# Where the square roots of the second feed-forward are taken: ScalarE or GpSimd

## The chip, the cores and the metric

One core of a Trainium2 chip runs the whole program. The metric is the device time of one launch in microseconds (us). TensorE (PE), VectorE (DVE), ScalarE (ACT) and GpSimd (POOL) each work through an instruction list of their own; SyncE (SP) issues most of the DMAs. They meet at semaphores.

## The reference

Two transformer layers on x of shape 4 x 1024 x 128, 16 heads of width 8. Layer 0 has attention by distances and a routed feed-forward. Layer 1, which the change touches, is:

```python
xn = _layernorm(x)
x = x + _L1_attn_ref(xn, ...) + _L1_ffn_ref(xn, ...)

# _L1_attn_ref: softmax(q k / sqrt(8)) over l, einsum 'blmh,blhd->blhd', out projection
# _L1_ffn_ref:
real = jnp.einsum('bti,io->bto', x, jnp.cos(theta + theta_noise))
imag = jnp.einsum('bti,io->bto', x, jnp.sin(phi + phi_noise))
return jnp.sqrt(real * real + imag * imag)
```

In the attention of layer 1 each query's value is multiplied by its own sum of weights, so only the row sums of the exponentials are wanted.

## The kernel before

The program has a long first part, 16 rounds of four heads of layer 0 (to about 975 us of the span), and then the attention of layer 1, which is one long loop: 4 batches b of 128 tiles s (16 heads x 8 blocks of 128 queries), 512 tiles in all. For each tile

- PE makes 128 x 1024 scores in one of three PSUM ring tiles (L1327),
- ACT takes the exponential into one of eight places `EX[k // 2][:, k % 2]` in SBUF (L1352, or L1348, which also makes the sum itself: every fifth tile, s = 16, 21, 26 and so on, outside the last batch),
- DVE folds the 1024 columns to a sum (L1360, `dve_fold`, "fold" below): both halves of the place are its inputs, so it reads two operands from SBUF. Tiles whose sum ACT makes have no fold.

`act_exp1` waits, at even s, until the folds of all tiles up to s - 7 are done: a place of EX is used again only then. PE can be three tiles ahead of ACT.

Beside this loop batch b + 1 is prepared while batch b runs, each step fixed to a tile number s by hand (`ATURN_AT`, `ADD_AT` and so on): DVE copies and adds at s = 20 and 30, adds the feed-forward of layer 0 at s = 31 to 46 (L1190 and L1199, one short instruction a tile, two operands from SBUF plus a scalar), measures and normalises, keeps q, k, v, and copies real and imaginary parts to `ri` at s = 114 and 126 (`dve_square_mix`). POOL gathers rows by indirect DMA (`pool_gather`), takes the deviation, splits q into parts (`pool_split_q1`) and squares and adds `ri` into `mag[b]` (`pool_powers`, twice a batch, L1302 and L1304). Batch 0 is prepared in the last round of layer 0. At the end of a batch the output projection of the attention is added: PE begins it at s = 36 of the next batch (`FWO_AT`), in the one PSUM tile `aux`, which DVE's step at s = 30 (`dve_add_att`, L1183) has to have emptied, and its first instructions are two matmuls for the bias (L1163). DVE adds the result at s = 40.

The roots are taken by `act_magnitudes`: at s = 16 of the last batch (`MAG_HEAD` = 2 heads of 8 tiles) ACT turns from exponentials to roots, takes four roots of 128 x 1024, and turns back. `pool_add_magnitudes` adds `mag[b]` to `X[b]` for each batch. Those of batches 0 and 1 follow at once, those of 2 and 3 after the projection of batch 2 (s = 40). SP stores the results of batches 0 to 2 from s = 55 on; DVE needs the last sum at s = 122.

In layer 0 POOL already takes some of the square roots by nine fp32 operations (`pool_roots`, L771 to L786): an integer seed, one multiplication, and a cubic, in place. Its DVE partner there reads PSUM.

Which of the two branches runs (`by_guard`) is decided by the data; the trace shows the fast one.

Of the kernel before, what the change touches and what calls it, by code (L numbers as in the profile page):

```python
# [19 lines left out]
I32 = mybir.dt.int32  # L20
# [5 lines left out]
P = 128  # L26
# [209 lines left out]
def build(nc, d):  # L236
    with ExitStack() as ctx, ExitStack() as scores_ctx, ExitStack() as room:
# [43 lines left out]
        with ExitStack() as own:  # L281
            late_room = lambda n, s, t=F32: own.enter_context(nc.sbuf_tensor(n, s, t))
            EX = [late_room(f"exp{i}", [P, 2, N]) for i in range(NT // 2)]
            X = [None] + [late_room(f"X{b}", [P, NT, D]) for b in range(1, B)]
            V1 = [None] + [late_room(f"V{b}", [P, NT, D]) for b in range(1, B)]
            mag = [None] + [late_room(f"mag{b}", [P, NT, D]) for b in range(1, B)]
            fatt = late_room("fatt", [P, N])

# [239 lines left out]
        def pool_deviation(pool, n, ready, done):  # L530
            pool.wait_ge(ready, n + 1)
            nc.gpsimd.tensor_tensor(rstd[:], mv[:, :, 1], power.to_broadcast([P, NT]), ALU.pow).then_inc(done, 1)  # L532
# [929 lines left out]
        def act_magnitudes(act):  # L1462
            for b in range(B):
                act.wait_ge(mag_half, 2 * (b + 1))
                nc.scalar.activation(mag[b][:, :, :], mag[b][:, :, :], ACT.Sqrt).then_inc(mag_root, 1)

        def pool_add_magnitudes(pool, o, b, after_end):
            pool.wait_ge(mag_root, b + 1)
            if after_end:
                o.emptied(pool, ("fwo", b))  # L1470
            else:
                pool.wait_ge(xn1_ready, NT * (b + 1))
            nc.gpsimd.tensor_tensor(X[b][:, :, :], X[b][:, :, :], mag[b][:, :, :], ALU.add).then_inc(mag_added, 1)
# [119 lines left out]
        FTURN_AT, ATURN_AT, AWO_AT, FWO_AT = 10, 18, 26, 36  # L1593
        ADD_AT, STATS1_AT, NORMAL_AT, TURN1_AT = 31, 47, 57, 68
        Q1_AT, K1_AT, SPLIT1_AT, V1_AT, MIX_AT = 79, 88, (92, 94, 96, 98), 97, (108, 120)
        MAG_HEAD, STORE1_HEAD, STORE_RESULT_HEAD = 2, 12, 6

        WEIGH_LAST_AT = [LAST_GROUP + GROUP * hi for _, hi in LAST_PARTS[:-1]]
        TURN_LAST_AT, KEEP_LAST_AT = [WEIGH_LAST_AT[0] + 4, H * NT - 2], [WEIGH_LAST_AT[0] + 5, H * NT - 4]
# [384 lines left out]
        @block.scalar  # L1984
        def _(act):
            act.dma_start(early["full"][:], d["early_full"]).then_inc(early_in, 16)
            act.dma_start(limit["full"][:], d["limit_full"]).then_inc(limit_in, 16)
            for i, (a, b) in enumerate((("theta", "theta_noise"), ("phi", "phi_noise"))):
                act.dma_start(ang[:, i, :], d[a]).then_inc(angles_in, 16)
                act.dma_start(noise[:, i, :], d[b]).then_inc(angles_in, 16)  # L1990
            act_first(act, first_order)

            def sines(act):
                act.wait_ge(reduced, 1)
                nc.scalar.activation(cs0[:].rearrange("p (a c) -> p a c", a=2), ang[:, :, :], ACT.Sin
                                     ).then_inc(trig_done, 1)

            def general(act):
                sines(act)
                general0(act, "act")  # L2000
                act_odds(act)
                for v in range(FIRST_JOBS, LAST_JOBS + 1):
                    act_tanh(act, general_order, v)
                act_magnitudes(act)
                for u in range(GROUPS):
                    general1(act, "act", u)

            def fast(act):
                o = fast_order
                sines(act)  # L2010
                for r in range(GROUPS):
                    if r:
                        for place in range(GROUP):
                            act_root_halves(act, o, r, place) if (r, place) == (1, GROUP - 1) else act_root(act, o, r, place)
                    else:
                        act_first_roots(act, o)
                    for place in range(GROUP):
                        if place == 2:
                            if r == FIRST_JOBS - 1:
                                act_odds(act)  # L2020
                            if FIRST_JOBS <= r <= LAST_JOBS:
                                act_tanh(act, o, r)
                        act_exp0(act, r, place) if r or place else act_first_exp(act)
                for b in range(B):
                    for s in range(H * NT):
                        if b == B - 1 and s == MAG_HEAD * NT:
                            act_magnitudes(act)
                        act_exp1(act, o, b, s)

            by_guard(act, general, fast)  # L2030

        @block.gpsimd
        def _(pool):
# [49 lines left out]
            def fast(pool):  # L2083
                o, chain, roots = fast_order, Chain(pool, pool_steps, 1), Chain(pool, newton_steps)
                store_sines(pool)
                pool_deviation(pool, 1, var_ready, std_ready)
                normalise0(pool, nc.gpsimd, 1)
                for r in range(GROUPS):
                    if 1 <= r < B:
                        pool_qk0(pool, o, chain, r)  # L2090
                        if r + 1 < B:
                            pool_deviation(pool, r + 1, var_ready, std_ready)
                            normalise0(pool, nc.gpsimd, r + 1)
                        if r == 1:
                            pool_roots(pool, o, roots, r, 1)
                        pool_sums0(pool, o, chain, r)
                    if FIRST_JOBS < r <= LAST_JOBS + 1:
                        pool_hidden(pool, r - 1)
                    if r == PLACE_ROUND:
                        pool_place(pool, o, chain)  # L2100
                    if r == ADD1_ROUND:
                        pool.wait_ge(y_stored, Y_ALL)
                        pool_gather(pool, 0)
                    if r == PLACE_ROUND + 1:
                        pool_scatter(pool, 2)
                        for place in range(1, GROUP - 1):
                            pool_roots(pool, o, roots, r, 1, place - 1, place)
                            pool.wait_ge(att_ready, GROUP * (r - 1) + place + 1)
                            pool_scatter(pool, 2 + place)
                    elif r == PLACE_ROUND + 2:  # L2110
                        pool_scatter(pool, 7)
                    if r > 1 and r != PLACE_ROUND + 1:
                        pool_roots(pool, o, roots, r, 1)
                    if r == FIRST_JOBS or r > PLACE_ROUND + 1:
                        pool_roots(pool, o, roots, r, 2, 0, 1)
                    if r:
                        pool_store_out(pool, r - 1)
                    if r == PLACE_ROUND:
                        pool_scatter(pool, 0)
                    if r == PLACE_ROUND + 1:  # L2120
                        pool_scatter(pool, 5)
                    if r == ADD1_ROUND:
                        pool_deviation(pool, 0, var1, std1)
                    if r == 2:
                        pool_roots(pool, o, roots, r, 2)
                    elif r > PLACE_ROUND + 1 or r == FIRST_JOBS:
                        pool_roots(pool, o, roots, r, 2, 1)
                    if FIRST_JOBS < r <= LAST_JOBS + 1:
                        pool_store_jobs(pool, o, r - 1)
                    if r == PLACE_ROUND:  # L2130
                        pool_scatter(pool, 1)
                    if r == PLACE_ROUND + 1:
                        pool_scatter(pool, 6)
                    pool_roots(pool, o, roots, r, 3)
                    if r == TURN1_ROUND:
                        roots.wait()
                        clear_stacks1(pool)
                pool_split_q1(pool, o, chain, 0)
                for i in range(2):
                    pool_powers(pool, o, chain, 0, i)  # L2140
                pool_store_out(pool, GROUPS - 1)
                pool.wait_ge(att_out, 32 * GROUPS)
                for b in range(1, B):
                    pool_gather(pool, b)
                    pool_deviation(pool, b, var1, std1)
                    pool_split_q1(pool, o, chain, b)
                    for i in range(2):
                        pool_powers(pool, o, chain, b, i)
                for b in range(B):
                    pool_add_magnitudes(pool, o, b, b < B - 1)  # L2150

# [299 lines left out]
```

## Time and profile before

| | us |
|---|---|
| median of 3 runs | 1465.37 (1465.34 to 1466.09) |
| profiled execution, its time | 1468.72 |
| profiled execution, its span | 1467.0 |
| ACT busy | 1428.0 (97%) |
| DVE busy | 1220.8 (83%) |
| PE busy | 1110.7 (76%) |
| POOL busy | 884.5 (60%) |

Times in the rows are counted from the start of the span. Durations overlap a little where an engine has one instruction in flight behind the other, so the distance between two starts says more than the durations. A timeline row of several instructions has its total and their number. In the layer 1 loop POOL is mostly idle and ACT is hardly ever.

### The profile page before, as it was taken

The page shows a single profiled execution, that of the slowest core. Times are in us where ns is not written, and L with a number is a line of the kernel's source. Part 1 is how long each engine was busy: PE and PEld are TensorE (multiplying, and loading weights), DVE is VectorE, ACT ScalarE, POOL GpSimd, SP SyncE. Part 2 cuts the span into 40 slices and gives each one's busy share as a digit, 9 for nine tenths or more (in the row PEclk, how much of TensorE's full clock was granted, in tenths as well). Part 3 has the DMA queues.
Part 4 walks back from the last instruction along what each step waited for, and adds up shares of the span by engine and source line. Part 5 has one row for each costly group of instructions (what it writes and reads, how often), then busy time and mean ns, then how long its engine had stood idle before and what let it go on. Part 6 is the DMA issues. An engine that isn't in the chain of part 4 may idle for free.

```text
span 1467.0 us, 22437 instructions
## 1 busy us (share of the span) xinstructions
PE 1110.7 (76%) x8231; PEld 445.9 (30%) x8260; DVE 1220.8 (83%) x2196; ACT 1428.0 (97%) x796; POOL 884.5 (60%) x656
## 2 busy tenths in 40 slices
PE   5587787888788888888887675777777677776766
PEld 2133224245143352452542311322223122221212
DVE  6998889978879879789788588838898898998886
ACT  3999999999999999999999999989999999999998
POOL 5188998878789898898898985933213023022100
PEclk8599988999999999899999897889999999999999
DMA  4942544222322235254353231034033033021020
GB/s 121 253 141 65 167 129 125 60 61 73 82 82 62 64 102 155 80 144 131 83 155 96 69 75 31 13 120 81 27 128 71 27 113 81 27 106 33 23 70 20
DMA packets 113185, 130.04 MB, mean 89 GB/s; under 512 B 42906, under 2 KB 81178, under 8 KB 113066
## 3 DMA queue, kind: packets, MB, share of 16 engines
q1 hardware_dynamic: 107738, 116.74, 29.5%
q0 software_dynamic: 4464, 11.09, 2.8%
q8 instruction: 67, 1.10, 0.3%
q10 hardware_dynamic: 864, 0.69, 0.2%
q14 instruction: 52, 0.43, 0.1%
HBM read 83.79 MB, written 44.70 MB: 88 GB/s over the span
## 4 chain that ended last, share of the span: by engine, by line
ACT 38%; POOL 27%; DVE 15%; issue 12%; PE 6%; DMA 2%; SPq 1%; ACTq 0%; DVEq 0%; POOLq 0%
ACT exp L1352 13%; ACT scores L830 11%; ACT scores L791 6%; DVE exp L1360 6%; DVE scores L737 6%; POOL scratch L775 3%; POOL scores L773 3%; ACT exp L1348 3%; PE pvb L718 3%; POOL gate L1098 3%; POOL scratch L784 3%; POOL scores L786 3%; POOL scratch L780 3%; ACT h L1091 2%; POOL scratch L777 1%
## 5 line engine op out<-in xcount | busy, mean ns | idle before, releaser
L737 DVE TENSOR_SCALAR scores<-ring 128x1024 f32<-128x1024 f32 x512 | 591.8, 1216 | 62.2 <-PE ring L703 58.9
L830 ACT ACTIVATE scores<-scores 128x8192 f32<-128x8192 f32 x63 | 438.9, 7020 | 0.2
L1352 ACT ACTIVATE exp<-ring 128x1024 f32<-128x1024 f32 x438 | 431.4, 1388 | 4.4 <-PE ring L1327 3.9
L718 PE MATMUL pvb<-scores,val 128*9 128x256 f32 x4096 | 338.3, 406 | 97.8 <-ACT scores L830 63.7
L1327 PE MATMUL ring<-stk 128*128 128x512 bf16 x995 | 300.9, 386 | 131.2 <-ACT exp L1352 103.4
L791 ACT ACTIVATE scores<-scores 128x7296 f32<-128x7296 f32 (+2 forms) x59 | 384.1, 6574 | 4.9 <-DVE scores L737 4.8
L1360 DVE SCALAR_TENSOR_TENSOR exp<-exp 128x512 f32<-128x512 f32 x438 | 322.3, 758 | 62.6 <-ACT exp L1352 55.6
L703 PE MATMUL ring<-stk 64*128 64x512 bf16 x1024 | 216.1, 419 | 59.2 <-DVE scores L737 45.4
L1327 PEld LDWEIGHTS ring<-stk 128*128 128x128 bf16 x1024 | 66.1, 97 | 341.7 <-ACT exp L1352 232.5
L703 PEld LDWEIGHTS ring<-stk 64*128 64x128 bf16 x1024 | 50.0, 94 | 303.4 <-DVE scores L737 182.3
L718 PEld LDWEIGHTS pvb<-scores,val 128*9 128x9 f32 x4096 | 65.8, 89 | 226.9 <-issue 223.5
L1059 PE MATMUL ring<-xjt,w 128*128 128x128 f32 x840 | 101.3, 285 | 10.9 <-issue 9.7
L1059 PEld LDWEIGHTS ring<-xjt,w 128*128 128x128 f32 x840 | 100.0, 201 | 12.3 <-issue 10.8
L1348 ACT ACTIVATE exp<-ring 128x1024 f32<-128x1024 f32 x74 | 100.0, 1354 | 0.2 <-PE ring L1327 0.2
L773 POOL TENSOR_TENSOR scores<-scores,scratch 128x896 f32<-128x896 f32 (+1 forms) x39 | 75.2, 1928 | 3.3
L784 POOL TENSOR_TENSOR scratch<-scratch 128x896 f32<-128x896 f32 (+1 forms) x39 | 75.2, 1927 | 3.3
L775 POOL TENSOR_TENSOR scratch<-scores,scratch 128x896 f32<-128x896 f32 (+1 forms) x39 | 75.2, 1929 | 3.1
L786 POOL TENSOR_TENSOR scores<-scores,scratch 128x896 f32<-128x896 f32 (+1 forms) x39 | 75.1, 1925 | 3.1
L1302 POOL TENSOR_TENSOR at<-at 128x1024 f32<-128x1024 f32 x8 | 17.4, 2176 | 93.2 <-DVE at L1298 93.2
L532 POOL TENSOR_TENSOR rstd<-mv,columns 128x8 f32<-128x8 f32 x7 | 11.7, 1674 | 100.7 <-DVE mv L528 100.7
L1084 DVE COPY h<-ring 128x384 f32<-128x384 f32 x70 | 39.0, 557 | 26.7 <-PE ring L1059 25.9
L780 POOL TENSOR_TENSOR scratch<-scratch 128x896 f32<-128x896 f32 (+1 forms) x39 | 60.3, 1546 | 0.0
(263 smaller groups left out, 1434.9 us busy)
## 6 DMA issues: line engine op xcount, KB each, us to landing
stk<-stack SPq DMA_DIRECT2D x192, 192.0 KB, 2.8
w<-in_w SPq DMA_DIRECT2D x39, 352.0 KB, 3.6
w<-in_w SPq DMA_DIRECT2D x39, 192.0 KB, 2.7
stack<-qp SPq DMA_DIRECT2D x7, 768.0 KB, 4.4
stack<-kp SPq DMA_DIRECT2D x7, 768.0 KB, 5.4
xj<-xg SPq DMA_DIRECT2D x10, 448.0 KB
yg<-xj POOLq DMA_DIRECT2D x10, 448.0 KB, 3.6
stack<-qp SPq DMA_DIRECT2D x7, 512.0 KB, 5.1
```

What stands on the lines that cost most here:

```text
L703: mm = nc.tensor.matmul(tile[:, cols], stk0[slot][side, K, j * P:(j + 1) * P], stk0[slot][side, Q, cols], start=True, stop=True)
L718: mm = nc.tensor.matmul(pvb[place % 2][32 * c:32 * c + VW, 0:256], val[place][:, j, :], S[place][:, j * N + c * 256:j * N + (c + 1) * 256] ...
L737: nc.vector.tensor_scalar(S[place][:, j * N:(j + 1) * N], tile, 1e-12, None, ALU.max).then_inc(o.release(("qk", group, place, j)), 1)
L773: chain.step(nc.gpsimd.tensor_tensor(x, x, y, ALU.mult))
L775: chain.step(nc.gpsimd.tensor_tensor(y, x, y, ALU.mult))
L791: nc.scalar.activation(part, part, ACT.Sqrt).then_inc(root_done, 1)
L830: nc.scalar.activation(S[place][:], S[place][:], ACT.Exp, scale=-1.0).then_inc(exp_done, 1)
L1059: mm = nc.tensor.matmul(tile[:, at_col:at_col + P], w13[:, slot_of(v, j), side, first:first + P], xjt[:, j * P:(j + 1) * P], start=True, s ...
L1327: mm = nc.tensor.matmul(out[:, cols], stk1[place][:, Q, i * P:(i + 1) * P], stk1[place][:, K, cols], start=True, stop=True)
L1348: nc.scalar.activation(EX[k // 2][:, k % 2, :], tile, ACT.Exp, scale=SCALE1, accum_out=den[n // GROUP % 2][:, n % GROUP, i:i + 1]).then_in ...
L1352: nc.scalar.activation(EX[k // 2][:, k % 2, :], tile, ACT.Exp, scale=SCALE1).then_inc(o.release(("qk1", n, i)), 1)
L1360: nc.vector.scalar_tensor_tensor(out=tile[:, k % 2, 0:N // 2], in0=tile[:, k % 2, 0:N // 2], scalar=1.0, in1=tile[:, k % 2, N // 2:N], op0 ...
```

## The change

ACT no longer takes the roots in the fast branch. POOL takes them by the nine operations of layer 0, now on whole tiles of 128 x 1024 with two scratch tiles of their own (8 KB a partition), each operation but one waiting for the one before. The roots of batch b - 1 stand between the gather and the deviation of batch b, those of the last batch after its powers and ahead of the four additions. POOL also waits there once for the last weighing matmuls of layer 0, whose SBUF space the scratch tiles share.

```diff
+            mag_y, mag_h = late_room("mag_y", [P, N]), late_room("mag_h", [P, N])
...
+        def pool_magnitudes(pool, chain, b):
+            pool.wait_ge(mag_half, 2 * (b + 1))
+            y, h, x = mag_y[:], mag_h[:], flat(mag[b])
+            chain.step(nc.gpsimd.tensor_scalar(y.bitcast(I32), x.bitcast(I32), -0.5, SEED_BITS, ALU.mult, ALU.add))
+            chain.wait()
+            chain.step(nc.gpsimd.tensor_tensor(x, x, y, ALU.mult))
+            chain.wait()
+            chain.step(nc.gpsimd.tensor_tensor(y, x, y, ALU.mult))
+            chain.wait()
+            chain.step(nc.gpsimd.tensor_scalar(h, y, CUBIC[0], 1.0, ALU.add, ALU.mult))
+            chain.wait()
+            chain.step(nc.gpsimd.tensor_scalar(y, y, CUBIC[2], CUBIC[3], ALU.add, ALU.mult))
+            chain.step(nc.gpsimd.tensor_tensor(h, h, h, ALU.mult))
+            chain.wait()
+            chain.step(nc.gpsimd.tensor_scalar(h, h, CUBIC[1], 1.0, ALU.add, ALU.mult))
+            chain.wait()
+            chain.step(nc.gpsimd.tensor_tensor(h, h, y, ALU.mult))
+            chain.wait()
+            nc.gpsimd.tensor_tensor(x, x, h, ALU.mult).then_inc(mag_root, 1)
...
-        MAG_HEAD, STORE1_HEAD, STORE_RESULT_HEAD = 2, 12, 6
+        STORE1_HEAD, STORE_RESULT_HEAD = 12, 6
...
-                        if b == B - 1 and s == MAG_HEAD * NT:
-                            act_magnitudes(act)
                         act_exp1(act, o, b, s)
...
                 pool.wait_ge(att_out, 32 * GROUPS)
+                pool.wait_ge(pv_done, CHG * GROUPS)
                 for b in range(1, B):
                     pool_gather(pool, b)
+                    pool_magnitudes(pool, roots, b - 1)
                     pool_deviation(pool, b, var1, std1)
                     pool_split_q1(pool, o, chain, b)
                     for i in range(2):
                         pool_powers(pool, o, chain, b, i)
+                pool_magnitudes(pool, roots, B - 1)
                 for b in range(B):
                     pool_add_magnitudes(pool, o, b, b < B - 1)
```

## Rows read from the trace of the kernel before

**Rows 1.** Busy time by engine in two stretches: window and length, engines, PEclk, DMA, GB/s
```profile
core 0: us, PE busy (x) PEld busy (x) DVE busy (x) ACT busy (x) POOL busy (x), PEclk, DMA share, GB/s
1095.00:1215.00 120.00, 89.83 (x357) 31.95 (x362) 106.49 (x280) 119.97 (x153) 25.93 (x17) 1.00 0.26 71
1351.00:1358.00 7.00, 0.65 (x3) 0.11 (x2) 1.45 (x6) 6.94 (x8) 4.25 (x2) 0.86 0.00 0
```

**Rows 2.** Timeline of ACT in the last batch: start, us, engine, line, operation
```profile
1338.72 12.57 ACT L1352 ACTIVATE exp<-ring 128x1024 f32<-128x1024 f32 x13
1351.32 1.28 ACT L1465 ACT_TABLE_LOAD   x1
1352.61 3.90 ACT L1465 ACTIVATE mag<-mag 128x1024 f32<-128x1024 f32 x4
...
1357.82 43.39 ACT L1352 ACTIVATE exp<-ring 128x1024 f32<-128x1024 f32 x47
```

**Rows 3.** Timeline of POOL, first two of the four splits of q, batch 1
```profile
1056.49 1.43 POOL L574 CAST qp<-ysh 128x1024 bf16<-128x1024 f32 x1 [22.44 <-DVE ysh L1244]
1058.01 2.45 POOL L576 TENSOR_TENSOR ysh<-ysh,qp 128x1024 f32<-128x1024 f32 x1
```

**Rows 4.** Timeline of DVE, the folds beside those splits and two after
```profile
1056.97 1.49 DVE L1360 SCALAR_TENSOR_TENSOR exp<-exp 128x512 f32<-128x512 f32 x1
...
1058.40 2.60 DVE L1360 SCALAR_TENSOR_TENSOR exp<-exp 128x512 f32<-128x512 f32 x1
...
1060.93 1.51 DVE L1360 SCALAR_TENSOR_TENSOR exp<-exp 128x512 f32<-128x512 f32 x1
...
1062.38 2.60 DVE L1360 SCALAR_TENSOR_TENSOR exp<-exp 128x512 f32<-128x512 f32 x1
...
1064.91 0.68 DVE L1360 SCALAR_TENSOR_TENSOR exp<-exp 128x512 f32<-128x512 f32 x1
...
1065.52 0.68 DVE L1360 SCALAR_TENSOR_TENSOR exp<-exp 128x512 f32<-128x512 f32 x1
```

**Rows 5.** Timeline of POOL, the additions of batches 2 and 3
```profile
1383.05 5.42 POOL L1473 TENSOR_TENSOR X<-X,mag 128x1024 f32<-128x1024 f32 x2 [24.66 <-DVE X L1414]
```

**Rows 6.** Timeline of DVE, the first fold beside those additions
```profile
1383.44 2.83 DVE L1360 SCALAR_TENSOR_TENSOR exp<-exp 128x512 f32<-128x512 f32 x1
```

**Rows 7.** Timeline of POOL where DVE has no fold to make
```profile
953.90 1.03 POOL L574 CAST qp<-ysh 128x1024 bf16<-128x1024 f32 x1
...
960.44 1.89 POOL L1302 TENSOR_TENSOR at<-at 128x1024 f32<-128x1024 f32 x1
...
1353.74 4.64 POOL L1473 TENSOR_TENSOR X<-X,mag 128x1024 f32<-128x1024 f32 x2 [12.17 <-ACT mag L1465]
```

**Rows 8.** Groups by form, POOL, a scalar step of the nine in layer 0
```profile
L771 POOL TENSOR_SCALAR scratch<-scores 128x896 int32<-128x896 int32 x32 | 30.0, 937 | 13.6 <-DVE scores L737 9.6 <-issue 1.6
```

**Rows 9.** Timeline of POOL, the instructions that the nine follow (batches 0, 1, 3)
```profile
1010.95 1.25 POOL L1139 DMA_INDIRECT yro<-yg,pos  x1 [0.30 <-issue]
...
1112.62 1.40 POOL L1139 DMA_INDIRECT yro<-yg,pos  x1 [0.30 <-issue]
...
1340.02 1.56 POOL L1304 TENSOR_TENSOR mag<-at 128x512 f32<-128x512 f32 x1
```

**Rows 10.** Timeline of DVE where the nine come to lie in batches 0 and 1
```profile
1012.18 0.35 DVE L1190 SCALAR_TENSOR_TENSOR X<-ysh,WT,X 128x128 f32<-128x128 f32 x1
1012.45 0.69 DVE L1360 SCALAR_TENSOR_TENSOR exp<-exp 128x512 f32<-128x512 f32 x1
...
1114.61 0.69 DVE L1360 SCALAR_TENSOR_TENSOR exp<-exp 128x512 f32<-128x512 f32 x1 [0.79 <-issue]
...
1127.35 1.22 DVE L1183 TENSOR_TENSOR X<-X,aux 128x1024 f32<-128x1024 f32 x1
```

**Rows 11.** Timeline of ACT: tile 46 of batch 0, tiles 37 to 40 of batch 1
```profile
1021.17 1.21 ACT L1348 ACTIVATE exp<-ring 128x1024 f32<-128x1024 f32 x1
...
1132.38 3.77 ACT L1352 ACTIVATE exp<-ring 128x1024 f32<-128x1024 f32 x4
```

**Rows 12.** Groups by form, PE, the bias matmuls in `aux`
```profile
L1163 PE MATMUL aux<-late_rows,fixed_full 128*128 128x512 f32 x26 | 12.4, 596 | 0.7 <-DVE fatt L1433 0.7
```

## The prediction

> **What bounds the kernel now.** I read the busy times by stretch first. From 1095 to 1215 us, one batch of the layer 1 loop, ACT is busy 119.97 of 120 us [rows 1]: the loop ends when ACT has made its 512 exponentials, so a microsecond taken from ACT is won, and one in which it waits is lost for good. DVE is busy 106.49 of the same 120 us and POOL 25.93: POOL has room by its own time, DVE has little. Then the timeline of ACT in the last batch shows the detour that the change removes [rows 2]. Last I read POOL and DVE side by side wherever POOL is busy in this loop [rows 3 to 6], because the nine operations must run there.
>
> **What is removed.** Tiles 3 to 15 of the last batch are the 13 exponentials from 1338.72 us. The 47 after the detour take 43.39 us, that is 0.92 us a tile. Tile 16 would start at 1338.72 + 13 x 0.917 = 1350.6 us and starts at 1357.82 [rows 2]. The detour costs 7.2 us: two table loads of 1.3 us, four roots in 3.90 us, and 0.7 us for the pipe. PE has nothing to do meanwhile and its granted clock falls (mean 0.86 in that window, so for part of it at 1.2 and not at 2.4 GHz, [rows 1]), but the 47 exponentials keep their pace, so the clock adds nothing. Sum so far: -7.2 us.
>
> The Trainium skill (ScalarE: Activation LUTs, What ACT_TABLE_LOAD costs) gives 2.66 us for each change of table, 1.28 of it the load and the rest a drain. By it the detour would be 2 x 2.66 + 3.90 = 9.2 us and the gain 2 us more. The trace agrees on the load, but shows 7.2 us in all; I go by the trace.
>
> **What is added: POOL's time.** Alone, an fp32 sum of two tiles takes 4.64 / 2 = 2.32 us, a square 1.89, a one-operand CAST 1.03 [rows 7]; the scalar steps of the nine take 0.937 at 896 columns [rows 8], so about 1.05 at 1024, next to the cast. Nine operations are four scalar steps, one square and four two-operand ones: 4.2 + 1.9 + 4 x 2.32 = 15.4 us a batch, without gaps. POOL has that time: in batch 0 from 1012.3 us on, in batches 1 and 2 from 1114.2 us and one batch later, in batch 3 from 1341.7 [rows 9]. The gathers stand ahead of the nine, so no DMA is later, and the wait for layer 0's matmuls adds nothing behind the wait for their stored result. Were that all, the change would win 7.2 us.
>
> **What is added: DVE's folds wait.** It isn't all. Beside a cast of POOL a fold takes 1.49 us and beside a two-operand step 2.60, against a start-to-start distance of 0.61 in folds that have POOL to themselves [rows 3, 4]. POOL's operation grows too: cast 1.03 to 1.43, pair of sums 4.64 to 5.42 [rows 3, 5, 7], where the fold takes 2.83 [rows 6]. So they take turns: each POOL operation runs whole, one fold gets in behind it, then the next operation. In the 7.9 us of the four splits DVE makes four folds [rows 4], where ACT needs about seven in that time. Turns hold for any DVE instruction with two SBUF operands, I take it: the short L1190 too.
>
> The Trainium skill (SBUF — State Buffer, Who interferes with whom) states the rule that speaks against this change: a VectorE instruction with two SBUF inputs and a GpSimd one that reads SBUF exclude each other for their whole length. It says that issue order decides, not that they alternate; were VectorE to win several turns in a row, the loss below would shrink towards the second rival.
>
> With turns, a fold lengthens the period by 0.4 to 0.45 us, a short L1190 by about 0.2. The chain of nine takes 15.4 + 9 x 0.43 = 19.3 us beside folds and lets through nine or ten DVE instructions. ACT makes 21 tiles in that time and can run ahead of the folds by 6 or 7. The four splits stayed within this slack; nine don't.
>
> *Batch 0.* The chain starts at 1012.4 us; DVE is at the fold of tile 34 [rows 9, 10]. It lies among the short additions, one a tile, so it gets through 34, add, 35, add, add (36 has no fold), 37, add, 38, add: nine turns. Half of them lengthen the period by 0.2 only, so the chain ends at 1012.4 + 15.4 + 4 x 0.45 + 5 x 0.2 = 1030.6, and fold 39, for which tile 46 waits, is done near 1031.4. Tile 46 starts at 1021.17 now [rows 11]: +10.2 us.
>
> *Batches 1 and 2.* The chain starts at 1114.2 us, fold 17 waits for it [rows 9, 10]. Turns: 17, 18, 19, 20, 22, 23, 24, 25; one turn is lost to the PSUM copy at tile 20, which needs none. The chain ends near 1132.8, folds 25, 27 to 30 are done at 1135.9, and only then comes L1183 (tile 30), which now starts at 1127.35 [rows 10]. It ends at 1137.1. PE stands at tile 36 until it has, then makes two bias matmuls of 0.6 us [rows 12] and the scores of tile 37, 0.6 us. Tile 37 starts near 1139 instead of 1132.38 [rows 11]: +6.6, and PE, now without lead, has the projection's matmuls among the next four tiles: I take +7 in each batch, +14 in both.
>
> *Batch 3.* The last L1304 ends at 1341.6 us [rows 9], the chain runs from 1342.0 to 1361.2 beside folds 1 to 9, and the additions of batches 0 and 1 follow, which lie in ACT's detour now [rows 7]: two more turns of 2.8 us, folds 10 and 11, done near 1367.3. Tile 18 waits for fold 11. Without the detour it would start at 1350.6 + 1.8 = 1352.5: +14.8, and the copy at tile 12 adds 0.6: +15.4.
>
> *Sum:* -7.2 + 10.2 + 14 + 15.4 = +32.4 us. The profiled span would be 1467.0 + 32.4 = 1499.4. The profiled execution's 1468.72 lies 3.35 above the median; the loss being the same on both, I predict 1465.37 + 32.4 = 1497.8 us. What is late next is DVE, with a backlog of six tiles after each chain; it clears it at 0.61 us a fold against 0.92 (more slowly beside the additions), before the steps at tile 57 and later, where PE needs its results. The deviation, behind the nine in POOL's list, now comes at tile 55, when the chain is over.
>
> **Bounds.** From below, the trace doesn't show whether a scalar step that is no cast shares turns with the fold. Nearest above is the cast, which does; I take that. If it doesn't, see the second rival. From above, each stall may be a tile or two longer: one more turn is up to 2.8 us in any of four batches, and PE's clock falls in each (it did in 7 us, [rows 1]) while in batches 0 to 2 PE has projections to make. Two turns and 1.5 us of slow PE in three batches are +10: 1508.
>
> **Rivals.** (1) *Faster.* All turns fit in the slack of ACT: decided where a chain leaves at most about six tiles unfolded. The four splits do fit [rows 4]; the nine would have to last under 12 us, or fold and POOL overlap. Then only -7.2 remains: 1458.2 us. Against it stand rows 3 to 6.
> (2) *Smaller loss.* The four scalar steps let folds pass, or DVE gets two folds in per turn. In 4.2 us a chain DVE makes up to seven folds, not four; with shorter periods that is some 4.5 us less stall a chain, 18 us in four: 1479.8 us.
> (3) *Larger loss.* PE, idle in each stall and slow after it, holds ACT further, or the backlog reaches the next step's deadline (q, k at tile 79 on): another +10 to +20, about 1512 us.
> (4) *It doesn't show:* the roots on POOL cost just what they save. This needs a loss of 7 us in four chains, under 2 each; nothing in the rows gives it.
>
> **How the numbers follow.** Forecast 0.72, (2) 0.15, (3) 0.08, (1) 0.04, (4) 0.01. The range runs from 1478 (rival 2) to 1508 (upper bound) and leaves (3), (1) and (4) out. About 0.2% (2.9 us) is what a measurement of this kernel tells from no change. Faster 0.04, same 0.01, slower 0.95.
>
> **What the profile would show.** ACT: no table load near 1351 us, but gaps or stretched starts behind each chain, in order 10, 7, 7 and 15 us. DVE: folds of 2.8 us beside POOL's two-operand steps, about 1.5 beside scalar steps, nine turns a chain. POOL: chains of 18 to 20 us; the granted clock dips once a batch. Wrong would be: folds of 0.7 us beside scalar steps (rival 2), no gap of ACT at all (rival 1), gaps that don't follow the chains (rival 3).

## The result and the profile after

The changed kernel takes 1495.24 us (median of 4, 1493.47 to 1497.07) against 1465.47 (median of 4) in the same session: ratio 1.0205, 95% interval 1.0193 to 1.0217, so 29.8 us slower. Its profiled execution has 1493.47 us and a span of 1491.8, 24.8 above the span before. It happens to be the fastest of its four runs, while the profiled execution before (1468.72) lies above all of its timed ones, so the two spans understate the difference.

The page's busy times are the first hint. POOL worked 74 us more than before (884.5 then), DVE 49 us more (1220.8 then) with the same 2196 instructions, ACT 6 us less:

```profile
PE 1124.5 (75%) x8260; PEld 445.7 (30%) x8260; DVE 1269.4 (85%) x2196; ACT 1422.3 (95%) x790; POOL 958.8 (64%) x692
```

An engine that gets busier with the same work is being held inside its instructions, and that is DVE here. What ACT waited for from just ahead of the layer 1 loop to its end (engine and line, released by, us in total, times, longest), the changed kernel:

```profile
ACT exp L1353 <- DVE exp L1361: 18.4, 9, 3.6
ACT exp L1353 <- PE ring L1328: 14.4, 6, 5.6
ACT exp L1349 <- DVE exp L1361: 2.7, 1, 2.7
ACT exp L1349 <- PE ring L1328: 0.2, 1, 0.2
```

and the kernel before:

```profile
ACT exp L1352 <- PE ring L1327: 3.9, 2, 2.1
ACT exp L1348 <- PE ring L1327: 0.2, 1, 0.2
```

Waits on DVE's folds were not there at all; waits on PE were 4.1 us. To place them I measure the loop by ACT's own sums, of which each batch has its first at tile 16 and its last at tile 121. These are the readings of the accumulator in the timeline of the changed kernel, tiles 16 and 121 of batch 0, the same of batches 1 and 2, and the last sum of all (the line numbers are one higher than before):

```profile
989.13 0.26 ACT L1349 ACTIVATION_READ_ACCUMULATOR exp<-ring 128x1 f32 x1
1094.92 0.65 ACT L1349 ACTIVATION_READ_ACCUMULATOR exp<-ring 128x1 f32 x1
1115.81 0.92 ACT L1349 ACTIVATION_READ_ACCUMULATOR exp<-ring 128x1 f32 x1
1220.95 0.64 ACT L1349 ACTIVATION_READ_ACCUMULATOR exp<-ring 128x1 f32 x1
1241.84 0.92 ACT L1349 ACTIVATION_READ_ACCUMULATOR exp<-ring 128x1 f32 x1
1346.97 0.65 ACT L1349 ACTIVATION_READ_ACCUMULATOR exp<-ring 128x1 f32 x1
1485.66 0.24 ACT L1349 ACTIVATION_READ_ACCUMULATOR exp<-ring 128x1 f32 x1
```

and three of the kernel before, the first, tile 121 of batch 2 and the last:

```profile
993.93 0.26 ACT L1348 ACTIVATION_READ_ACCUMULATOR exp<-ring 128x1 f32 x1
1330.49 0.64 ACT L1348 ACTIVATION_READ_ACCUMULATOR exp<-ring 128x1 f32 x1
1461.51 0.24 ACT L1348 ACTIVATION_READ_ACCUMULATOR exp<-ring 128x1 f32 x1
```

From such rows, in us (batch 3 from tile 121 of batch 2 to the last sum; "between" the two stretches from tile 121 to the next tile 16):

| | batch 0 | batch 1 | batch 2 | batch 3 | between | loop |
|---|---|---|---|---|---|---|
| before | 97.85 | 98.47 | 98.47 | 131.02 | 41.77 | 467.58 |
| changed | 105.79 | 105.14 | 105.13 | 138.69 | 41.78 | 496.53 |
| difference | +7.9 | +6.7 | +6.7 | +7.7 | 0 | +28.95 |

The whole difference of the medians, 29.8 us, lies in this loop but for 0.8. What lies around the loop (median minus the loop of the profiled execution) is 997.9 and 998.7 us. From one profiled execution to another tile 16 of batch 0 comes at 989 to 995 us, which is why spans are a poor measure here and this table is a good one: where nothing disturbs them, batches 1 and 2 repeat to 0.1 us and batch 0 to 0.4.

Batch 1 shows what happens. The chain on POOL:

```profile
1117.27 1.05 POOL L1471 TENSOR_SCALAR mag_y<-mag 128x1024 int32<-128x1024 int32 x1
1118.40 2.67 POOL L1473 TENSOR_TENSOR mag<-mag,mag_y 128x1024 f32<-128x1024 f32 x1
1121.14 2.68 POOL L1475 TENSOR_TENSOR mag_y<-mag,mag_y 128x1024 f32<-128x1024 f32 x1
1123.91 1.37 POOL L1477 TENSOR_SCALAR mag_h<-mag_y 128x1024 f32<-128x1024 f32 x1
...
1132.86 2.68 POOL L1486 TENSOR_TENSOR mag<-mag,mag_h 128x1024 f32<-128x1024 f32 x1
```

and DVE beside it:

```profile
1117.75 1.10 DVE L1361 SCALAR_TENSOR_TENSOR exp<-exp 128x512 f32<-128x512 f32 x1 [0.75 <-ACT exp L1353]
...
1118.78 2.83 DVE L1361 SCALAR_TENSOR_TENSOR exp<-exp 128x512 f32<-128x512 f32 x1
...
1121.55 2.83 DVE L1361 SCALAR_TENSOR_TENSOR exp<-exp 128x512 f32<-128x512 f32 x1
...
1124.31 1.51 DVE L1361 SCALAR_TENSOR_TENSOR exp<-exp 128x512 f32<-128x512 f32 x1
...
1125.75 1.21 DVE L1158 COPY att_t<-aux 128x1024 f32<-128x1024 f32 x1
```

One DVE instruction gets in for each operation, here eight folds and one copy for the nine. A fold takes 0.68 us alone; beside an operation it is held until that operation is done: 2.83 us beside two operands, 1.51 beside a scalar step. These are the turns of [rows 3, 4] and [rows 6]. The last row is the surprise. PE needs this copy (tile 20) for the output projection of layer 0 at tile 26, and it starts 9.9 us after ACT's sum of tile 16 (1115.81), where it started 5.3 us after it before (1117.91 against 1112.66). PE and ACT, the same batch:

```profile
1127.02 3.78 PE L1164 MATMUL aux<-late_rows,fixed_full 128*128 128x512 f32 x4 [3.13 <-DVE att_t L1158]
```

```profile
1131.69 3.92 ACT L1353 ACTIVATE exp<-ring 128x1024 f32<-128x1024 f32 x4 [5.62 <-PE ring L1328]
...
1142.19 3.77 ACT L1353 ACTIVATE exp<-ring 128x1024 f32<-128x1024 f32 x4 [0.92 <-PE ring L1328]
```

ACT stops at tile 27, not at tile 34 or 37, with nothing wrong in the folds it waits for. The bias matmuls (two in the program, four rows in the profile) took 3.78 us. The same four of the kernel before, with the clock at full speed:

```profile
1120.58 1.88 PE L1163 MATMUL aux<-late_rows,fixed_full 128*128 128x512 f32 x4
```

PE had idled for 3.1 us, and from 1127 to 1131 us its granted clock was 0.50, the level of 1.2 GHz:

```profile
1127.00:1131.00 4.00, 3.98 (x5) 1.47 (x6) 4.00 (x5) 0.00 (x0) 3.83 (x3) 0.50 0.02 4
```

(columns as in [rows 1]). From the first bias matmul to ACT's tile 27 it is 4.67 us here and was 2.35 before (1120.58 to 1122.93): the clock lengthens this stall by 2.3 us.

Batch 3, the additions included, is the plain case of folds. ACT:

```profile
1347.06 15.22 ACT L1353 ACTIVATE exp<-ring 128x1024 f32<-128x1024 f32 x16
1365.66 1.94 ACT L1353 ACTIVATE exp<-ring 128x1024 f32<-128x1024 f32 x2 [3.38 <-DVE exp L1361]
1368.54 1.94 ACT L1353 ACTIVATE exp<-ring 128x1024 f32<-128x1024 f32 x2 [0.95 <-DVE exp L1361]
1372.28 1.94 ACT L1353 ACTIVATE exp<-ring 128x1024 f32<-128x1024 f32 x2 [1.80 <-DVE exp L1361]
1377.78 1.94 ACT L1353 ACTIVATE exp<-ring 128x1024 f32<-128x1024 f32 x2 [3.56 <-DVE exp L1361]
1383.28 1.94 ACT L1353 ACTIVATE exp<-ring 128x1024 f32<-128x1024 f32 x2 [3.56 <-DVE exp L1361]
```

Two exponentials, then a wait of two turns, again and again: ACT runs at the pace of POOL.

### The profile page after: what moved, and what is told of

It is laid out like the page before. It is cut to its first block, busy times and chain, and to the rows that moved or that the text cites. A ratio compares the mean times of both kernels' runs of the same rounds, so it can differ in the third digit from the quotient of the medians.

```text
span 1491.8 us, 22496 instructions
## 1 busy us (share of the span) xinstructions
PE 1124.5 (75%) x8260; PEld 445.7 (30%) x8260; DVE 1269.4 (85%) x2196; ACT 1422.3 (95%) x790; POOL 958.8 (64%) x692
## 4 chain that ended last, share of the span: by engine, by line
ACT 52%; DVE 20%; issue 12%; PE 7%; POOL 6%; DMA 1%; SPq 0%; another core or an unknown queue 0%; ACTq 0%; DVEq 0%; POOLq 0%
ACT scores L831 18%; ACT scores L792 16%; ACT exp L1353 11%; DVE exp L1361 10%; DVE scores L738 6%; PE pvb L719 3%; ACT exp L1349 3%; PE ring L704 2%; ACT h L1092 2%; ACT L831 1%; ACT L792 1%; DVE X L1191 1%; POOL scores L774 1%; POOL scratch L776 1%; PE ring L1328 1%
## 5 line engine op out<-in xcount | busy, mean ns | idle before, releaser
L1328 PE MATMUL ring<-stk 128*128 128x512 bf16 x1024 | 313.3, 393 | 132.8 <-ACT exp L1353 107.1
L1361 DVE SCALAR_TENSOR_TENSOR exp<-exp 128x512 f32<-128x512 f32 x438 | 363.0, 857 | 39.7 <-ACT exp L1353 36.0
L1060 PE MATMUL ring<-xjt,w 128*128 128x128 f32 x840 | 98.2, 279 | 10.6 <-issue 9.5
L1060 PEld LDWEIGHTS ring<-xjt,w 128*128 128x128 f32 x840 | 96.8, 196 | 12.1 <-issue 10.5
L1099 POOL TENSOR_TENSOR gate<-gate,h 128x2688 f32<-128x2688 f32 x10 | 59.4, 5942 | 0.9
```

What stands on the lines that cost most here:

```text
L1060: mm = nc.tensor.matmul(tile[:, at_col:at_col + P], w13[:, slot_of(v, j), side, first:first + P], xjt[:, j * P:(j + 1) * P], start=True, s ...
L1328: mm = nc.tensor.matmul(out[:, cols], stk1[place][:, Q, i * P:(i + 1) * P], stk1[place][:, K, cols], start=True, stop=True)
L1361: nc.vector.scalar_tensor_tensor(out=tile[:, k % 2, 0:N // 2], in0=tile[:, k % 2, 0:N // 2], scalar=1.0, in1=tile[:, k % 2, N // 2:N], op0 ...
```

## The experiments

All times beside the kernel before on the same chip (its medians there 1465.1 to 1466.0 us). "Loop" is the last column of the table above, for each run's profile.

**Nothing in place of the roots.** The chains are left out.

```diff
                     pool_gather(pool, b)
-                    pool_magnitudes(pool, roots, b - 1)
...
-                pool_magnitudes(pool, roots, B - 1)
```

> The changed kernel with the nine operations left out: nobody takes the roots of the second feed-forward, and the four additions of POOL stay. It measures what taking the detour from ACT is worth when nothing comes in its place. Theory (turns between POOL's operations and DVE's folds make the loss): only the 7.2 us of the detour go, ratio to the kernel before 0.995, about 1458 us, and ACT shows no gap longer than before. Rival (the detour was not worth 7.2 us, or removing it already upsets the loop): 1465 us or more.

Measured: 1461.63 us, ratio 0.9978 (0.9968 to 0.9987), loop 463.48. Faster, but by 3.5 us in the medians and 4.1 in the loop, not by the 7.2 that the theory gave. Batches 0 to 2 are those of before to 0.15 us; batch 3 has 127.05. ACT, batch 3:

```profile
1343.87 1.94 ACT L1353 ACTIVATE exp<-ring 128x1024 f32<-128x1024 f32 x2 [1.01 <-DVE exp L1361]
1347.23 101.14 ACT L1353 ACTIVATE exp<-ring 128x1024 f32<-128x1024 f32 x110 [1.43 <-DVE exp L1361]
```

The additions of batches 0 and 1, which the detour used to cover, now come right behind the powers of batch 3, four reading operations in a row, and that already costs ACT 2.4 us. So a kernel without the detour comes near the 7.2 us only if the additions find another place.

**The same time on POOL, without reading.**

```diff
-            chain.step(nc.gpsimd.tensor_scalar(y.bitcast(I32), x.bitcast(I32), -0.5, SEED_BITS, ALU.mult, ALU.add))
...
-            nc.gpsimd.tensor_tensor(x, x, h, ALU.mult).then_inc(mag_root, 1)
+            for k in range(12):
+                chain.step(nc.gpsimd.memset(mag_y[:], 0.0))
+                chain.wait()
+            nc.gpsimd.memset(mag_h[:], 0.0).then_inc(mag_root, 1)
```

> The changed kernel with each chain of nine operations replaced by 13 memsets of 128 x 1024 (1.15 us each in this kernel's rows, so 15 to 16 us a chain, the time that the nine would need alone), in the same places with the same waits; the roots are not taken. POOL is busy and late by as much, but reads nothing from SBUF. Theory (what stops DVE is an operation of POOL that reads SBUF while the fold reads two operands): folds keep 0.68 us beside the memsets and the time is that without the nine, about 1458 us. Rival (POOL being busy, whatever it does, delays the loop, by its queue or by any access to SBUF): folds of 1.5 us beside the memsets; with 13 turns a chain the loss is at least that of the changed kernel, 1495 us or more.

Measured: 1458.48 us, ratio 0.9948 (0.9932 to 0.9965), loop 461.10, that is 6.5 us less than before. POOL and DVE in batch 1:

```profile
1111.43 12.08 POOL L1471 MEMSET mag_y<- 128x1024 f32 x12
```

```profile
1113.77 0.69 DVE L1361 SCALAR_TENSOR_TENSOR exp<-exp 128x512 f32<-128x512 f32 x1 [0.22 <-ACT exp L1353]
...
1114.68 0.69 DVE L1361 SCALAR_TENSOR_TENSOR exp<-exp 128x512 f32<-128x512 f32 x1 [0.21 <-ACT exp L1353]
...
1115.30 1.22 DVE L1158 COPY att_t<-aux 128x1024 f32<-128x1024 f32 x1
```

The memsets came out at 1.0 us each, so a chain is 13 us, and not the 15 to 16 that were expected (the nine take 18.3 in the changed kernel), but no fold beside them is longer than 0.69. POOL being busy for 13 us more in each batch cost nothing; reading does. This is the decisive run. The Trainium skill (SBUF — State Buffer, Who interferes with whom) says just this, that a GpSimd instruction which only writes doesn't meet a two-operand VectorE one. It also gives what the detour is worth by the end of batch 3: 124.41 us here, 6.6 less than before.

**Operation by operation, spread over the tiles.**

```diff
+        def pool_spread(pool, o, chain, steps, b, places):
+            for s in places:
+                o.emptied(pool, ("qk1", *tile_at(b, s)))
+                chain.wait()
+                chain.step(next(steps))
...
-                    pool_magnitudes(pool, roots, b - 1)
+                        pool_spread(pool, o, roots, steps[1], 1, (18, 25))
```

> All roots are taken on POOL by the same nine operations, but one at a time: those of batch 0 ahead of the loop (scratch in ysh and yro), the other 27 each behind a tile of the loop, six in batch 1, six in batch 2, fifteen in batch 3, with six to eight tiles or more between most of them, and the additions likewise. Theory (a POOL operation delays the folds by 1 to 2 us, and ACT loses only when the backlog passes about six tiles): folds of 1.5 to 2.8 us appear singly, no ACT gaps of several us, so the detour's 7.2 us are won: 1458 to 1461 us, ratio 0.995 to 0.997. Rival (each POOL operation costs ACT time wherever it stands, 29.6 + 7.2 = 37 us for 36 operations, about 1 us each): near 1490 us.

Measured: 1474.7 us, ratio 1.0062 (1.0045 to 1.0079), loop 473.29. Twenty microseconds of the loss are gone with the same 36 operations, so an operation has no fixed price. But neither is it free, and the forecast missed by 14 us: batches 1 and 2 have 102.68 and 103.36 us, with all of the excess at tiles 102 to 111, behind two operations (tiles 97 and 104) that met DVE's split of k; batch 3 has 127.84, 3.4 over the memset run; and what lies around the loop is 1001.4 us instead of 997.5 in that session (see below, e8_spread_more).

**The copy at tile 20 moved ahead of the chain.**

```diff
-                            if s == ATURN_AT:
+                            if s == ATURNS_AT[b]:
...
+        ATURNS_AT = [18, 13, 13]
```

> The changed kernel, with the transposition of the attention's output of layer 0 and its copy by DVE moved from tiles 18 and 20 to tiles 13 and 15 in batches 1 and 2, so that the copy is made before the chain of nine starts at about tile 16. It tells apart what ACT waits for in these two batches. Theory (several limits lie close together: the copy at tile 20, the folds seven tiles back, the emptying of aux at tile 30): the PE gap of 3.1 us before the bias matmuls at tile 26 goes, the loss moves to the next limit, tiles 34 to 37, and the sum stays within 1.5 us of the changed kernel a batch, 1492 to 1495 us. Rival (the copy at tile 20 alone makes the loss of 6.7 us a batch): about 13 us less, 1482 us.

Measured: 1496.99 us, ratio 1.0215 (1.0198 to 1.0232), loop 500.80. It lies 2 us above its forecast and far from the rival's 1482, but it doesn't answer cleanly. The transposition at tile 13 needs `aux` from DVE's step at tile 12, and DVE still has the backlog of the powers there:

```profile
1115.42 1.12 PE L1150 MATMUL aux<-fixed_full,at 128*128 128x128 f32 x4 [3.41 <-DVE fatt L1398]
```

That wait is new: 25.05 and 24.15 us between the batches instead of 20.89. Inside batches 1 and 2 the loss is 4.2 and 5.8 us instead of 6.7. ACT's long wait at tile 27 went, and waits of 0.7 to 1.5 us at tiles 26, 28, 30 and 37 came (in batch 2 three of 1.3 to 3.0 us).

**The chain moved behind the copy.**

```diff
                     pool_gather(pool, b)
+                    if b > 1:
+                        o.emptied(pool, ("aturn", b))
                     pool_magnitudes(pool, roots, b - 1)
```

> The changed kernel, but in batches 1 and 2 POOL waits with the nine until DVE has made its copy at tile 20 (the copy for which PE was seen to wait before the bias matmuls at tile 26). This tells apart again what the stall in these batches hangs on; the first try moved the copy and brought a wait of its own. Theory (the stall is the backlog of DVE, and whichever of its duties is due next shows it): the wait moves to the aux tile at tile 36 or to the folds, and a batch loses 5 to 9 us still, 1494 to 1500 us in all. Rival (the copy at tile 20 alone): the loss of 6.7 us a batch falls under 2, about 1485 us.

Measured: 1499.06 us, ratio 1.0231 (1.0214 to 1.0248), batches 1 and 2 at 108.30 and 106.94 us: 9.8 and 8.5 us lost instead of 6.7. This is the clean test of the same question. PE, batch 1:

```profile
1140.80 3.78 PE L1164 MATMUL aux<-late_rows,fixed_full 128*128 128x512 f32 x4 [6.42 <-DVE X L1184]
```

The wait sits at tile 36 for DVE's step at tile 30, the place that the prediction had named, and is longer; the bias matmuls behind it are again at half the pace. The copy at tile 20 isn't the cause, only the first duty that the backlog makes late.

**Twice as many instructions, half as long.**

```diff
+            cut = [slice(width * k, width * (k + 1)) for k in range(PIECES)]
+            ts, tt = nc.gpsimd.tensor_scalar, nc.gpsimd.tensor_tensor
-            chain.step(nc.gpsimd.tensor_tensor(x, x, y, ALU.mult))
+            chain.step(each(lambda c: tt(x[:, c], x[:, c], y[:, c], ALU.mult)))
```

> The changed kernel with each of the nine operations and each of the four additions cut into two of half the columns, in the same places. POOL moves the same bytes in twice the instructions and is busy longer. Theory (POOL and DVE take turns by instruction, one fold gets in after each): 18 folds a chain in some 23 to 25 us instead of nine or ten in 19, so in batches 1 and 2, where 20 folds are needed in that time, the stall all but goes; batch 3 keeps 1 to 4 us; about 1460 to 1468 us. Rival (the loss follows POOL's busy time or its bytes, not its instruction count): as the changed kernel or more, 1495 to 1502 us.

Measured with PIECES = 2: 1483.37 us, ratio 1.0122 (1.0105 to 1.0139), loop 485.12: 11.4 us of the loss gone, though POOL's chain in batch 1 grew from 18.3 to 23.1 us. The rival fell, but the forecast missed by 15 us too. Batches 1 and 2 lose 2.9 us each (6.7 with whole operations), batch 3 10.9 over the 124.41 of the memset run (14.3) where 1 to 4 were expected, and batch 0, with 7.5 (7.9), gained almost nothing; why it didn't is not shown.

**Four times as many.** The same with PIECES = 4.

> The same with four pieces for each operation and addition, 256 columns each: 36 instructions a chain. Theory of turns by instruction: a fold gets in about every 1.0 to 1.1 us, against a need of one in 1.15 us in batches 1 and 2 and one in 0.92 in batch 3; no ACT gap of over 1 us anywhere, so the detour's 7.2 us are won: 1457 to 1461 us, faster than the kernel before. Rival (busy time or bytes): 1500 us or more. A second rival: short instructions let DVE in but cost POOL so much at 0.1 us or more apiece that the chain reaches the next duties of POOL (deviation at tile 55): 1465 or more.

Measured: 1475.23 us, ratio 1.0064 (1.0048 to 1.0081), loop 476.59, chains of 29.6 us in batch 1. It is better again, and the chain is 11 us longer than in the changed kernel: the loss follows the number of turns that DVE gets in a given time, not POOL's time. But it missed its forecast by 14 us. POOL, batch 1, and three folds beside it:

```profile
1122.11 3.99 POOL L1486 TENSOR_TENSOR mag<-mag,mag_y 128x256 f32<-128x256 f32 x4
```

```profile
1126.58 1.21 DVE L1361 SCALAR_TENSOR_TENSOR exp<-exp 128x512 f32<-128x512 f32 x1
...
1127.71 1.20 DVE L1361 SCALAR_TENSOR_TENSOR exp<-exp 128x512 f32<-128x512 f32 x1
...
1130.67 0.87 DVE L1361 SCALAR_TENSOR_TENSOR exp<-exp 128x512 f32<-128x512 f32 x1
```

A fold of 1.2 us is still longer than ACT's tile of 0.92, so in batch 3, where every tile has one, 7.6 us stay. Batches 1 and 2 lose 1.6 us each. And in batch 0, which loses 4.7, the second rival happened, at one place: the chain ended at 1041.8 us, the deviation behind it was late, and ACT has a gap of 3.4 us there.

**The spread placement mended.** Five operations each in batches 1 and 2, and ACT takes sums in the last batch too.

```diff
-    return n < HEADS - H and 12 <= s < 124 and s % 5 == 1 or n >= HEADS - GROUP and ...
+    return n < HEADS - GROUP and 12 <= s < 124 and s % 5 == 1 or n >= HEADS - GROUP and ...
```

> The spread kernel with its misplaced operations moved. It had lost 4.2 and 4.9 us in batches 1 and 2 at tiles 97 to 110, where an operation met DVE's split of k and the copy of v, and 4.4 in batch 3. Now five operations in each of batches 1 and 2, none between tiles 73 and 106, 17 operations and the additions in batch 3 at every fourth or fifth tile from 12 on, and ACT makes every fifth sum in batch 3 too (tiles to 95), which takes 17 folds from DVE. Theory (loss only where DVE's backlog passes what the next duty allows): no gap in batches 1 and 2, at most 2 us in batch 3: 1458 to 1462 us. Rival (each operation costs ACT about 0.3 us wherever it stands, the 36 of the first try having cost some 13 us): 1470 to 1475 us.

Measured: 1464.02 us, ratio 0.9989 (0.9979 to 0.9998), loop 463.46. Batches 0 to 2 have 97.61, 98.49 and 98.50 us, with the ten operations in batches 1 and 2 costing nothing; batch 3 has 127.12, 2.7 over the memset run, of which some 1.4 are ACT's 16 additional sums (an estimate, by the price of a sum in the next runs). So the loop won 4.1 us with all roots taken. The median won only 1.9, short of its forecast of 1458 to 1462 us: what lies around the loop is 1000.6 us instead of 998.4 in that session. The nine operations of batch 0 stand there, ahead of the loop. That they are the cause fits e11_spread_best, which has none there, and ACT's gaps at tiles 10 to 15 of batch 0, where the kernel before has none:

```profile
986.20 4.69 ACT L1355 ACTIVATE exp<-ring 128x1024 f32<-128x1024 f32 x5 [0.50 <-DVE exp L1363]
992.37 1.02 ACT L1355 ACTIVATE exp<-ring 128x1024 f32<-128x1024 f32 x1 [1.48 <-PE ring L1330]
```

**More sums on ACT, and their price.** In both runs `s % 3 == 1` instead of `s % 5 == 1`, up to tile 95 of the last batch; in the first the 36 operations all behind tiles of the loop, in the second nothing else.

> All roots on POOL again, operation by operation behind tiles of the loop, but none ahead of it (the nine of batch 0 ahead of the loop had delayed DVE's copy for the last group of layer 0: 0.5 and 1.5 us of ACT gaps before tile 16). ACT makes every third sum instead of every fifth, in all four batches (tiles 12 to 123, in the last to 95), which takes some 15 folds a batch off DVE (27 in the last) at under 0.1 us of ACT each. Six operations a batch from tile 66 on and three in the next batch at tiles 16, 20, 24. Theory (a POOL operation costs ACT nothing while DVE's backlog stays small): the 6.6 us of the detour are won and 2 to 4 us given for the sums: in the loop 462 to 466 us against 467.6, in all 1460 to 1463 us, faster than the kernel before. Rival (POOL's reads cost DVE and through it ACT in any place): 1466 us or more.

> The kernel before with nothing changed but that ACT makes every third sum instead of every fifth, as in the run above; the roots stay on ACT. It gives the price of the sums alone. Theory: ACT bounds the loop, each sum costs it under 0.1 us and folds taken from DVE win nothing: 1467 to 1469 us. Rival (DVE's share is what holds the loop in batches 0 to 2, and relief there wins time): 1463 us or less, and then what the run above wins is not the roots'.

Measured: 1466.98 us, ratio 1.0010 (1.0001 to 1.0019), and 1472.61 us, ratio 1.0053 (1.0040 to 1.0066). Both lie above their forecasts. The 73 additional sums cost 6.6 us, 0.09 us each. The price of one was as expected; the totals in the two forecasts (2 to 4 us, 1 to 3 us) were summed too low. So the spread kernel isn't faster than before. Between these two kernels, though, only the place of the roots (and of the additions) differs, and POOL's wins 5.6 us.

**All in the loop, sums as before.**

> The last placement: all 36 operations on POOL one by one behind tiles of the loop, none ahead of it, none between tiles 75 and 106 of a batch, ACT's sums every fifth tile as in the kernel before and in the last batch up to tile 95 too. Batches 0, 1 and 2 take 4, 6 and 6 operations, the last takes 20 and the four additions, one about every fourth tile. Theory: the loop costs as little as in e8_spread_more or 1 to 2 us more (463.5 to 465.5 us from the first sum of ACT to the last, against 467.6), and what lies ahead of it is 2 to 3 us shorter than there: 1461 to 1464 us, ratio to the kernel before 0.996 to 0.999. Rival (24 actions in the last batch outrun what DVE has spare there, 35 to 40 us): gaps of several us in the last batch, 1466 us or more.

Measured: 1466.3 us, ratio 1.0006 (0.9997 to 1.0015), loop 467.36: no gain, and the time that its rival named. With no operation ahead of the loop what lies around it is 998.9 us, 1.6 less than in e8_spread_more. But batches 0 and 1 lost 0.8 and 0.3 us, most of it at tiles 92 to 101, where none of the placed operations stands (the nearest are at 75 and 106), so what brings it there is not shown; and batch 3 has 129.81 us, 5.4 over the memset run (some 1.4 of it the 16 sums again), with 24 reading operations in it. From 1330 to 1460 us DVE is busy 120.46 us (before: 103.06): its spare time is nearly used up (columns as in [rows 1]).

```profile
1330.00:1460.00 130.00, 87.24 (x311) 24.18 (x318) 120.46 (x252) 125.52 (x159) 54.53 (x26) 0.97 0.12 34
```

## Why the prediction was right, and where it wasn't

The forecast of +32.4 us (1497.8) stands against 29.8 measured.

- *The detour, -7.2 us.* Measured -6.6 (batch 3 with memsets, 131.02 to 124.41). The reading was right at its place: from the last sum of batch 2 to the start of tile 16 it is 27.33 us before and 19.99 with memsets, 7.3 apart. But 0.7 us comes back at tile 37, beside the bias matmuls of the projection, where ACT loses 1.2 us with memsets and 0.5 before. The 9.2 us that would follow from the 2.66 us a change of table in the Trainium skill (ScalarE: Activation LUTs, What ACT_TABLE_LOAD costs) are further off: in the trace of the kernel before, each of the two loads (1351.32 and 1356.53 us) starts within 0.03 us of the end of the work ahead of it, and the next instruction within 0.01 us of the end of the load.
- *DVE takes turns with any POOL operation that reads, scalar steps included.* Held as put: 2.83, 1.51 and, beside the square, 2.37 us; the bound chosen for scalar steps (like the cast) was right, and the rival with the smaller loss fell on it. That reading is the cause, and not POOL's time, is shown by the memsets; that the unit is the instruction, by the halves and quarters. The size of that gain was overrated each time, by 15 and 14 us.
- *Batch 0, +10.2.* Measured +7.9. The step that failed is that a short L1190 takes a turn of its own like a fold ("the short L1190 too"). It waits like one, but then the fold behind it gets in before POOL's next operation:

```profile
1011.05 2.46 DVE L1191 SCALAR_TENSOR_TENSOR X<-ysh,WT,X 128x128 f32<-128x128 f32 x1
...
1013.43 0.68 DVE L1361 SCALAR_TENSOR_TENSOR exp<-exp 128x512 f32<-128x512 f32 x1
...
1014.04 2.24 DVE L1191 SCALAR_TENSOR_TENSOR X<-ysh,WT,X 128x128 f32<-128x128 f32 x2
```

- *Batches 1 and 2, +7 each.* Measured +6.7 each, with the mechanism right and the place wrong. I had let ACT stop at tile 34 for folds and at tile 37 for `aux`; it stopped at tile 27, where PE waited for the copy at tile 20. I had counted that copy as a lost turn and not asked who waits for it. Moving either side (e4_early_turn, e5_late_chain) moved the wait and kept the loss, so the size came from the backlog and agreed by more than luck, but the agreement to 0.3 us is luck: of a stall of 5.6 us the lower clock makes 2.3, which stood only in the upper bound (as 1.5 us) and in no step, and the bias matmuls were put at 1.2 us, two instructions by their mean in [rows 12], where the profile has four in 1.88 us at full clock.
- *Batch 3, +15.4 beside the detour's -7.2.* Measured 138.69 - 124.41 = +14.3. Eleven turns, then the pairs of exponentials; the 15.4 hold to 1.1 us. This term and the detour's are told apart by the memset run alone.
- *Sum:* 7.9 + 13.4 + 14.3 - 6.6 = 29.0 us in the loop, 29.8 in the medians.
- *The rival "faster"* needed the chain to fit in ACT's slack. Placed whole it doesn't; spread singly it nearly does, and the loop is then 4.1 us shorter than before, of which the medians show 1.9.

Open: whether a placement exists that wins the full 6.6 us. The busy time of DVE in e11_spread_best speaks against it as long as the fold reads two operands; the fastest kernel here that takes the roots on POOL (e8_spread_more) is 0.1% faster than before. Nor was it tried to take the chain away in one batch alone; the shares of the batches are read from the profiles.

## What to carry to other kernels

Before moving work to GpSimd because it is idle, list the VectorE instructions with two SBUF operands that will run beside it: each reading GpSimd instruction holds one of them for its own length, and what counts is how many such turns come in a row against the slack of the engine that bounds the kernel. Then ask of every VectorE duty in that stretch who waits for it, for the stall appears at the first one due, which may be a small copy for TensorE and not the work that is being held. If the work must go there, cut it short or spread it; work that only writes costs nothing, as far as the memsets here show.

## What was not expected of the hardware

- 13 memsets of 128 x 1024 in a row left two-operand folds at 0.69 us, while each of the whole reading operations beside them makes 1.5 to 2.8.
- A short two-operand DVE instruction (0.27 us from its start to the next) and the fold behind it pass together between two POOL operations that are 0.08 us apart; POOL's next operation then took 1.57 us instead of 1.37.
- Cutting a POOL operation into four raised a chain's time from 18.3 to 29.6 us (batch 1) and still took 20 us off the kernel.
- Four fp32 bias matmuls took 3.78 us at a granted clock of 0.50, after PE had waited 3.1 us (batch 1) or 6.4 us (e5_late_chain), against 1.88 at the full clock.
